# A two-block transformer and graph-attention kernel: first V spread through a mask over all partitions, four turned exponentials, identity products in TensorE's early holes, and a new order of the work

## The reference

```
cmod = silu(c) @ w_ada + b_ada            # six vectors per batch: shift, scale, gate, twice
x_mod = ln(x) * (1 + scale) + shift
k, q, v = split(x_mod @ w_qkv)
w = softmax((q / 8) k^T)                  # per batch and head, 32 x 32
x = x + gate * ((w v) @ w_proj + b_proj)
x = x + gate2 * (gelu(modulate(ln(x)) @ w_mlp1 + b_mlp1) @ w_mlp2 + b_mlp2)
```

```
self = concat(x, q_exp) @ W_self.T + b_self       # q_exp is zeroed where a row of x sums to 0
A = adj or its transpose, columns 0 to 19; label_bias = A @ w_bias + b_bias
aff = (self Wq)(self Wk)^T / sqrt(8), masked where A.sum(-1) == 0, + label_bias
output += softmax(aff) @ kv @ Wout + bout          # for each d
result = x + relu(self + output of both directions)
```

## Time and profile before

| what | value |
|---|---|
| runs | 101.66, 102.17, 102.39 us; median 102.17 us |
| profiled run | 101.14 us, span 99.3 us |
| PE busy | 83.0 us (84%) |
| PEld busy | 57.8 us (58%) |
| DVE busy | 76.3 us (77%) |
| ACT busy | 65.9 us (66%) |
| POOL busy | 65.5 us (66%) |
| DMA | 5.04 MB, nearly all of it in the first 17 us, and the stores at the end |

### The profile page before, as it was taken

How to read it: one execution, slowest core, us unless ns; L and a number is a source line. 1 busy time by engine, 2 the same in 40 slices (tenths; PEclk the granted TensorE clock), 3 DMA queues, 4 the chain that set the end, 5 groups by cost and what they waited for, 6 DMA issues and landing times.

```text
span 99.3 us, 4622 instructions
## 1 busy us (share of the span) xinstructions
PE 83.0 (84%) x1894; PEld 57.8 (58%) x1894; DVE 76.3 (77%) x209; ACT 65.9 (66%) x130; POOL 65.5 (66%) x118
## 2 busy tenths in 40 slices
PE   3996898448887598997989999998999999978730
PEld 3985675244455256863755666656665857856520
DVE  1698598629999999998467994775279786999990
ACT  1928679995872717672662788899953299997520
POOL 6758799995008970999946867990201999966700
PEclk9999589999999999999999999999999999999998
DMA  2947992000000000000000000000000000000033
GB/s 48 297 145 304 436 400 81 0 3 10 3 7 0 7 0 0 7 0 0 7 0 0 0 7 0 7 0 7 0 7 3 7 0 7 10 0 7 7 106 106
DMA packets 2532, 5.04 MB, mean 51 GB/s; under 512 B 336, under 2 KB 1872, under 8 KB 2256
## 3 DMA queue, kind: packets, MB, share of 16 engines
q1 hardware_dynamic: 2080, 4.23, 11.8%
q10 hardware_dynamic: 432, 0.52, 1.5%
HBM read 4.23 MB, written 0.52 MB: 48 GB/s over the span
## 4 chain that ended last, share of the span: by engine, by line
PE 31%; DVE 25%; ACT 15%; POOL 12%; issue 12%; ACTq 2%; DVEq 0%; POOLq 0%
DVE rden_T L964 5%; PE ps_p L613 5%; PE ps_p L679 5%; POOL Vz L477 4%; PE ps_s L667 4%; ACT Vz L778 3%; PE ps_p L701 3%; PE ps_p L552 2%; PE ps_p L590 2%; DVE E L953 2%; DVE neg_max L942 2%; POOL rstd L455 2%; ACT Kb L726 2%; ACT hidden L731 2%; DVE tok L981 2%
## 5 line engine op out<-in xcount | busy, mean ns | idle before, releaser
L784 ACT ACTIVATE PT<-ps_p 128x512 f32<-128x512 f32 x24 | 14.1, 595 | 9.5 <-PE ps_p L679 7.6
L778 ACT ACTIVATE Vz<-V_turned 20x384 f32<-20x384 f32 (+4 forms) x40 | 18.0, 455 | 1.7 <-DVE V_turned L862 0.9
L520 POOL TENSOR_TENSOR E<-E,neg_max 128x320 f32<-128x320 f32 x16 | 11.6, 730 | 11.3 <-DVE neg_max L937 10.4
L679 PE MATMUL ps_p<-ident,E 128*128 128x128 f32 x96 | 15.0, 281 | 1.9 <-DVE tok L971 0.8
L679 PEld LDWEIGHTS ps_p<-ident,E 128*128 128x128 f32 x96 | 10.4, 141 | 5.2 <-issue 4.4
L528 POOL TENSOR_SCALAR Kb<-k_raw,cols,head_mask 128x240 f32<-128x240 f32 (+1 forms) x24 | 12.1, 517 | 0.5 <-ACT k_raw L744 0.5
L731 ACT ACTIVATE hidden<-ps_p,cols 128x384 f32<-128x384 f32 (+1 forms) x12 | 6.3, 543 | 5.9 <-PE ps_p L608 5.8
L448 POOL TENSOR_SCALAR var_eps<-meanvar 128x2 f32<-128x2 f32 (+2 forms) x7 | 1.4, 194 | 13.0 <-DVE meanvar L801 12.7
L929 DVE TENSOR_TENSOR E<-ps_s,bias_dir 128x320 f32<-128x320 f32 x16 | 7.7, 484 | 2.4 <-PE ps_s L667 2.3
L608 PE MATMUL ps_p<-xm,w_rest_sb 128*128 128x384 f32 (+1 forms) x24 | 8.6, 467 | 0.5 <-DVE yT L976 0.5
L964 DVE RECIPROCAL rden_T<-ps_p 128x128 f32<-128x128 f32 x8 | 7.4, 941 | 1.9 <-PE ps_p L696 1.9
(11 more groups left out here) (98 smaller groups left out, 190.7 us busy)
## 6 DMA issues: line engine op xcount, KB each, us to landing
tok<-in_adj SPq DMA_DIRECT2D x1, 1408.0 KB, 5.7
w_rest_sb<-in_w_rest SPq DMA_DIRECT2D x1, 1088.0 KB, 7.9
xT<-in_xT SPq DMA_DIRECT2D x1, 512.0 KB, 8.7
x_tok<-in_x_tok ACTq DMA_DIRECT2D x1, 320.0 KB, 4.1
w_ada_sb<-in_w_ada SPq DMA_DIRECT2D x1, 256.0 KB, 4.3
out<-x_tok SPq DMA_DIRECT2D x1, 256.0 KB, 2.4
w_qkv_sb<-in_w_qkv SPq DMA_DIRECT2D x1, 192.0 KB, 3.7
out<-x_tok SPq DMA_DIRECT2D x1, 192.0 KB, 2.1
```

Of the source, the lines that this page charges most:

```text
L520: pool.tensor_tensor(e, e, neg_max[:, i % 3, :].unsqueeze(2).broadcast_to([P, H, M]), ALU.add)\
L679: ins = pe.transpose(ps[:, j * P:(j + 1) * P], E[:, i % 3, j * HI:(j + 1) * HI, :], ident[:, :])
L778: act.activation(Vz[rows, g0 * UB:g1 * UB, d, :, q * C:(q + 1) * C], V_turned[layer + d][rows, g0 * UB:g1 * UB, :, :], ACT.Copy).then_inc( ...
L784: act.activation(PT[:, i % 2, :, :], psum_of(("turn", i))[:, :].rearrange("p (j t) -> p j t", t=P), ACT.Exp)\
```

## The change

Five things are changed together.

1. The spread of V in layer 0 writes all 128 partitions: ACT copies `V_turned` with the per-partition scale `quad_mask[:, q]`, which is one on the partitions of quarter q and zero on the others. So the two fills of `Vz` for d = 0 (one on ACT, one on POOL) are gone, and the spread waits for the mask instead of for the filled `Vz`. Layer 1 writes as before. (A path that does this spread on POOL is added too, but `POOL_SPREADS` is empty.)
2. `PT` has four buffers instead of two (`PT_RING`), so `exp` of unit i waits for `values` of unit i-4.
3. `fill` entries name the entry that comes next on PE; they wait for its bank and write identity products there. There are now seven products in five entries: three before (xnT, 0), one each before (cmod, 1), (xnT, 1), (xnT, 2) and (k, 2). Before there were two in one entry.
4. `biases` moves to the head of ACT's sequence; both fills of d = 1 leave their place between label steps 10 and 11: the first goes to POOL's start, behind the fill of `E1`'s padding, the second behind label step 0.
5. `ORDER` and `BANKS` are new as a whole. Unit 7's `turn`, `exp` and `values` and with them (proj, 2) come after the second piece's (mlp1); (x2tok, 0) and (x2tok, 1) move behind `scores` 23, with `relu` 1, `relu` 3 and `ysum` 3.

```diff
+PT_RING = 4
...
-    ("zero", ("values", 0, 0)), ("masks", 0), ("stats", (0, 0)), ("zero", ("values", 0, 1)), ("silu", 0),
-    ("dense", ("cmod", 0)), ("rstd", (0, 0)), ("apply", 0), ("stats", (0, 1)), ("take", (("cmod", 0), 0)),
-    ("rstd", (0, 1)), ("apply", 1), ("zero", ("ones", 0)), ("dense", ("xnT", 0)), ("take", (("xnT", 0), 0)),
...
+    ("zero", ("pad",)), ("masks", 0), ("zero", ("values", 1, 0)), ("stats", (0, 0)), ("silu", 0), ("stats", (0, 1)),
+    ("dense", ("cmod", 0)), ("biases", 0), ("rstd", (0, 0)), ("rstd", (0, 1)), ("apply", 0),
+    ("fill", (3, "dense", ("xnT", 0))), ("dense", ("xnT", 0)), ("apply", 1), ("take", (("cmod", 0), 0)),
+    ("stats", (0, 2)), ("fill", (1, "dense", ("cmod", 1))), ("dense", ("cmod", 1)), ("take", (("xnT", 0), 0)),
...
+    ("sub", 1), ("dense", ("v", 3)), ("scores", 2), ("take", (("v", 2), 0)), ("spread", (0, 0, 0, 1)),
+    ("spread", (0, 1, 0, 3)), ("exp", 0), ("spread", (0, 0, 0, 3)), ("take", (("k", 2), 2)), ("take", (("v", 3), 0)),
+    ("max", 2), ("turn", 1), ("sub", 2), ("label", 0), ("zero", ("ones", 0)), ("take", (("k", 2), 3)),
+    ("spread", (0, 0, 0, 0)), ("take", (("k", 2), 0)), ("dense", "qz"), ("values", 0), ("recip", 0), ("mult", 0),
+    ("zero", ("values", 1, 1)), ("label", 1), ("label", 2), ("exp", 1), ("values", 1), ("scores", 3),
...
+    ("take", (("mlp1", 1, 2), 0)), ("sub", 7), ("dense", ("k1", 0, 0)), ("take", (("k1", 0, 0), 0)),
+    ("dense", ("mlp1", 1, 1)), ("dense", ("v1", 0, 0)), ("take", (("v1", 0, 0), 0)), ("take", (("mlp1", 1, 1), 0)),
+    ("keys", (0, 0)), ("edges", 0), ("turn", 7), ("dense", ("q1", 0, 0)), ("spread", (1, 0, 0, 2)), ("exp", 7),
+    ("take", (("q1", 0, 0), 0)), ("dense", ("mlp2", 1)), ("dense", ("k1", 0, 1)), ("dense", ("v1", 0, 1)),
+    ("values", 7), ("scores", 8), ("take", (("mlp2", 1), 0)), ("take", (("mlp2", 1), 1)), ("dense", ("rowsum", 1)),
+    ("take", (("k1", 0, 1), 0)), ("recip", 7), ("mult", 7), ("selfb", 0), ("badd", 8), ("max", 8),
+    ("dense", ("proj", 2)), ("take", (("rowsum", 1), 0)), ("dense", ("self", 1)), ("dense", ("q1", 0, 1)),
...
-ACT_ZEROS = [("values", 0, 0)]
+POOL_SPREADS = []
+
+ACT_ZEROS = []
...
-        PT = sb("PT", [P, 2, HJ, P])
+        PT = sb("PT", [P, PT_RING, HJ, P])
...
-            def keep_up(count):
+            def keep_up(count, ps):
...
-                    pe.matmul(ps_s[:, 0, 0:P], ident[:, :], ident[:, :], start=True, stop=True)
+                    pe.matmul(ps[:, 0:P], ident[:, :], ident[:, :], start=True, stop=True)
+
+            def fill(count, stage, i):
+                if stage == "scores":
+                    if i:
+                        pe.wait_ge(scores_read, i)
+                    keep_up(count, ps_s[:, 0, :])
+                else:
+                    name = i if stage == "dense" else (stage, i)
+                    wait_free(name)
+                    keep_up(count, psum_of(name))
...
-                    act.wait_ge(vz_ready[d], 1)
-                    rows = slice(QUAD * q, QUAD * q + (M if layer else S))
-                    act.activation(Vz[rows, g0 * UB:g1 * UB, d, :, q * C:(q + 1) * C],
-                                   V_turned[layer + d][rows, g0 * UB:g1 * UB, :, :], ACT.Copy).then_inc(v_spread, 1)
+                    place = Vz[:, g0 * UB:g1 * UB, d, :, q * C:(q + 1) * C]
+                    turned_v = V_turned[layer + d][:, g0 * UB:g1 * UB, :, :]
+                    if layer:
+                        act.wait_ge(vz_ready[d], 1)
+                        rows = slice(QUAD * q, QUAD * q + M)
+                        act.activation(place[rows], turned_v[rows], ACT.Copy).then_inc(v_spread, 1)
+                    else:
+                        act.wait_ge(masks_ready, 1)
+                        act.activation(place, turned_v, ACT.Copy, scale=quad_mask[:, q:q + 1]).then_inc(v_spread, 1)
                 elif stage == "exp":
                     act.wait_ge(turned, i + 1)
-                    if i >= 2:
-                        act.wait_ge(values_ready, i - 1)
+                    if i >= PT_RING:
+                        act.wait_ge(values_ready, i - PT_RING + 1)
```

More of the change, by code:

```diff
@@ L119 @@
-    ("turn", 3), ("max", 4), ("sub", 4), ("recip", 2), ("stats", (1, 0)), ("scores", 5), ("spread", (0, 3, 0, 2)),
-    ("exp", 3), ("max", 5), ("mult", 2), ("label", 6), ("turn", 4), ("sub", 5), ("exp", 4), ("values", 3),
-    ("values", 4), ("rstd", (1, 0)), ("take", (("x1tok", 0), 0)), ("turn", 5), ("dense", ("xn2T", 0)), ("recip", 3),
-    ("recip", 4), ("label", 7), ("mult", 3), ("mult", 4), ("scores", 6), ("take", (("xn2T", 0), 0)),
-    ("dense", ("proj", 1)), ("take", (("xn2T", 0), 1)), ("dense", ("mlp1", 0, 2)), ("exp", 5), ("max", 6),
@@ L124 @@
-    ("take", (("proj", 1), 0)), ("values", 5), ("take", (("mlp1", 0, 2), 0)), ("take", (("proj", 1), 1)),
-    ("recip", 5), ("dense", ("mlp1", 0, 1)), ("dense", ("mlp1", 0, 0)), ("take", (("mlp1", 0, 0), 0)),
-    ("take", (("mlp1", 0, 1), 0)), ("mult", 5), ("dense", ("x1tok", 1)), ("sub", 6), ("stats", (1, 1)),
-    ("dense", ("mlp1", 0, 3)), ("dense", "qz"), ("label", 8), ("scores", 7), ("turn", 6), ("max", 7),
-    ("take", (("mlp1", 0, 3), 0)), ("dense", ("mlp2", 0)), ("label", 9), ("rstd", (1, 1)), ("sub", 7),
@@ L174 @@
-    ("ya", 2), ("ya", 3), ("badd", 20), ("values", 16), ("max", 20), ("recip", 16), ("mult", 16),
-    ("spread", (1, 2, 1, 1)), ("take", (("sbtok", 0), 0)), ("values", 17), ("scores", 21), ("turn", 18),
-    ("turn", 19), ("dense", ("x2tok", 1)), ("recip", 17), ("ya", 0), ("ya", 1), ("mult", 17), ("badd", 21),
-    ("scores", 22), ("ysum", 3), ("ysum", 0), ("ysum", 1), ("max", 21), ("sub", 20), ("badd", 22), ("relu", 1),
-    ("spread", (1, 2, 1, 2)), ("spread", (1, 2, 1, 0)), ("spread", (1, 2, 0, 1)), ("sub", 21),
@@ new lines @@
+    ("dense", ("k", 3)), ("recip", 1), ("mult", 1), ("dense", ("proj", 0)), ("take", (("k", 3), 3)),
+    ("take", (("k", 3), 1)), ("turn", 2), ("exp", 2), ("max", 3), ("sub", 3), ("take", (("k", 3), 2)),
+    ("take", (("k", 3), 0)), ("scores", 4), ("take", (("proj", 0), 0)), ("take", (("proj", 0), 1)),
+    ("dense", ("x1tok", 0)), ("max", 4), ("turn", 3), ("label", 3), ("stats", (1, 0)), ("label", 4),
+    ("rstd", (1, 0)), ("values", 2), ("spread", (0, 2, 0, 0)), ("spread", (0, 3, 0, 3)), ("exp", 3),
@@ new lines @@
+    ("dense", ("q", 3)), ("label", 5), ("sub", 4), ("turn", 4), ("recip", 2), ("mult", 2), ("spread", (0, 2, 0, 2)),
+    ("values", 3), ("take", (("x1tok", 0), 0)), ("dense", ("xn2T", 0)), ("take", (("q", 3), 0)), ("recip", 3),
+    ("take", (("xn2T", 0), 0)), ("exp", 4), ("values", 4), ("scores", 5), ("take", (("xn2T", 0), 1)),
+    ("dense", ("mlp1", 0, 2)), ("label", 6), ("recip", 4), ("mult", 3), ("mult", 4), ("dense", ("proj", 1)),
+    ("max", 5), ("sub", 5), ("spread", (0, 3, 0, 2)), ("take", (("mlp1", 0, 2), 0)), ("dense", ("mlp1", 0, 1)),
@@ new lines @@
+    ("dense", ("mlp1", 0, 3)), ("take", (("mlp1", 0, 3), 0)), ("take", (("proj", 1), 0)),
+    ("take", (("mlp1", 0, 1), 0)), ("scores", 6), ("take", (("proj", 1), 1)), ("dense", ("mlp1", 0, 0)),
+    ("dense", ("x1tok", 1)), ("turn", 5), ("take", (("mlp1", 0, 0), 0)), ("stats", (1, 1)), ("max", 6),
+    ("dense", ("mlp2", 0)), ("sub", 6), ("label", 7), ("rstd", (1, 1)), ("take", (("x1tok", 1), 0)), ("turn", 6),
+    ("take", (("mlp2", 0), 0)), ("scores", 7), ("take", (("mlp2", 0), 1)), ("spread", (0, 3, 0, 0)),
@@ L187 @@
+    ("exp", 23), ("values", 23), ("ya", 6), ("ya", 7), ("recip", 23), ("mult", 22), ("mult", 23), ("ysum", 6),
+    ("ysum", 7), ("dense", ("x2tok", 2)), ("take", (("x2tok", 2), 0)), ("relu", 6), ("relu", 5), ("relu", 7),
 ]
@@ L209 @@
[L209 to L213 removed]
+    ("cmod", 0): 0, ("xnT", 0): 1, ("cmod", 1): 2, ("k", 0): 3, ("xnT", 1): 0, ("v", 0): 1, ("q", 0): 2,
@@ L771, in _ @@
                     ins.then_inc(xn_act, 1)
-                elif stage == "spread":
+                elif stage == "spread" and not on_pool(i):
                     layer, c, d, q = i
```

194 lines of the change are left out of this document (97 added, 97 removed), and 10 rows, old and new, of the table BANKS.

## The result

The changed kernel took **96.07 us** (median of four runs, 95.43 to 96.36) against 101.95 us for the kernel before (101.66 to 102.39): ratio 0.9411, 95% interval 0.9349 to 0.9473. Timed again in a later job, unaltered, it stood at 0.9483 (0.942 to 0.9547), so the gain is 5.2 to 5.9 us. The forecast was 99.3 us with a range from 97.0 to 101.9: the sign was right, the size off by half.

A forecast was written before the change was run, and what follows sets the result against it. It saw a changing bound: waits in the first 22 us, then DVE, PE, ACT, PE, PE with ACT, DVE. Gains of 2.5 + 0.3 + 0.1 = 2.9 us gave 99.3 us on the median, range 97.0 to 101.9.

The forecast's parts named there:

- the price of the mask on ACT: Layer 0's spreads on ACT: the scale operand adds 0.09 us each, 0.7 us for eight, before the first values.
- The bound of the first 22 us: Up to 22 us all engines wait for each other; largest hole, PE 2.06 and DVE 1.93 us, is for late biases.
- Start: Before ACT's second apply: first rstd about 4.2 us, first modulated chunk 0.9 us later, second apply 0.9 us earlier.
- ACT to the first values: ACT from second apply to chunk 0's last spread: 9.2 us plus 0.4 of gaps, values 0 2.7 us earlier.
- the clock: PE at 10 to 13 us: fills keep the clock from 0.50, worth 0.7 us of PE, counted at nothing.
- DVE's stage: Up to the third mlp input: DVE, 98% busy, hands the lead on less 0.7 us of waits; 2.5 us left.
- Labels: POOL's label path: two fills leave it, 3.9 us less, bias_dir about 4 us earlier, no gain in itself.
- PE's stages: From 38.8 to 79.5 us: same PE entries but one exchange, only idle can change; 0.3 us gained.
- The blocked third piece: Rival, chance 0.10: values 7 and proj 2 behind mlp2 of piece 1 make piece 2's mlp2 1.9 us late: 104.1 us.
- End: Last units: moving x2tok behind scores 23 gains 0.5 us, relus and ysum 3 lose 0.4; net 0.1 gained.
- three signs of a wrong forecast: values 0 after 20 us, PE idle over 2.5 us between 37 and 77, or scores 23 to last relu growing over 1 us.
- PE has more room: Rival, chance 0.12: all PE idle from 38.8 us goes (1.4 us), the last units give 0.9 instead of 0.1: 97.1 us.

The follow-up runs named there:

- b_mask: Kernel before with layer 0's spread through the mask (128 partitions, scale operand), both d = 0 fills gone, order otherwise the same: ratio 0.9983.
- a_nofill: Changed kernel without its seven identity (fill) products, the warm-up products at the start kept: ratio 0.9498 to the kernel before.
- the two load experiments: Changed kernel with one more reciprocal on DVE before recip 2: 0.9546; with one more identity product on PE before each of scores 3, 4, 5: 0.9485.
- b_biases: Kernel before with one entry moved, biases to the head of ACT's sequence: ratio 0.9729, 2.8 us faster.
- b_zero_early: Kernel before with the two d = 1 fills of Vz moved to before label steps 0 and 1: ratio 0.9988.
- b_relu_late: Kernel before with relu 1, 0, 3, 4 and 2 moved behind mult 21, ahead of ysum 5: ratio 1.0044.

## Why the prediction was wrong, point by point

Three terms of the sum failed: the price of the mask on ACT was put at 0.7 us and cost nothing; a wait of DVE was charged to the end, which it didn't reach; and PE's waits in the last units were left out. The points in order:

**The bound of the first 22 us: right.** The hole behind `biases` was a real one. *Start:* `rstd` at 4.22 us (4.2 forecast), `apply` 0 at 5.42 (5.5). The six fill records took 0.92 us and not 1.4, so the first modulated chunk was 0.44 us late, not 0.9. ACT's second `apply` began at 8.75 (8.7).

**ACT to the first values: mis-sized by 1.0 us, and the term is the price of the mask.** I forecast 9.2 us of work and 0.4 of gaps; it was 8.56 and none. `values` 0 came 3.68 us earlier for the forecast 2.7. I had counted the instructions rightly: 27 in the old stretch and 24 in the new, with one exponential, one key take, one spread and `biases` fewer and three key takes more. The term that failed is the 0.7 us for the scale operand of eight spreads. Their records did grow: 415 ns for 307 at 128 columns, 526 for 408, 624 for 520, that is 0.10 to 0.12 us against my 0.09, with the width going from 32 partitions to 128 as well. The rule of the Trainium skill (ScalarE: Activation LUTs, What ACT_TABLE_LOAD costs) puts a per-partition pointer operand at about 93 ns; the trace is 11 to 25 ns above it. But a longer record is not a later successor. In the changed kernel a masked spread of 128 columns is followed 0.29 us after its start and one of 256 columns after 0.40 us; the unmasked ones of the kernel before were followed after 0.21 to 0.33 and 0.31 to 0.44. The same sequence with and without the mask took 7.13 and 7.30 us (b_mask). At nothing for the mask the sum gives 8.5 us of work, and 8.56 was measured.

The 0.4 us of gaps is the other part. Of the old order's 1.7 us of ACT idle 0.88 was one wait for POOL's `neg_mean`, 0.60 one for PE's products at the clock of 0.50, and the rest small stops, mostly beside unmasked spreads. None of them is in the new profiled run. I counted the clock at nothing, since "ACT sets the pace". ACT does wait for PE where the early products are slow: 1.9 us in a_nofill, 1.77 us in the unaltered kernel's second profiled run. So the clock should have stood in the sum as a risk. How much of it the identity products take away is not shown.

**DVE's stage: this step failed.** I took 0.7 us off the lead ("2.5 us left") for waits around `rstd` (1, 1). The wait for `rstd` did not come: the take of x1tok 1 (35.70) follows `sub` 6 without a stop. Another one of the size came just ahead, at `stats` (1, 1), for PE's transposes:

```profile
33.32 0.69 DVE L838 BATCH_NORM_STATS2 stats<-ps_p 128x6 f32<-128x128 f32 x3 [0.87 <-PE ps_p L584]
...
35.70 0.87 DVE L846 SCALAR_TENSOR_TENSOR xn_tok<-ps_p,meanvar,rstd 128x128 f32<-128x128 f32 x3
```

From its first reciprocal to mlp2 of piece 0 DVE idled 1.21 us for 0.43 before, so it did lose about what I took off. (Over the whole stage the two look alike, 1.19 and 1.24 us, only because 0.76 of the old one is the end of the wait for `biases`.) What was wrong is that this loss reaches the end. DVE waited there for PE, and PE was busy without a stop from 30.15 to 35.45 us; over the stage PE idled 0.55 us less than before. That DVE paces the rest of the stage fits the two load experiments. From 2.7 to 2.5 was forecast, from 3.58 to 4.13 of PE's idle it went: 0.75 us of the miss. The other fault is of method: I carried DVE's lead from stage to stage and subtracted frictions, when PE's idle time (12.44 us in all before) was the account from which every gain had to be paid. Nor is much of a start's lead lost behind: from `values` 0 to the last relu's end the kernel before takes 75.6 us, b_biases 76.1, the changed kernel 73.7 and a_nofill 73.5, whether `values` 0 stands at 21.11, 18.86, 17.43 or 19.1.

**Labels: right.** `bias_dir` is done at 43.69 us (44 forecast). That it is no gain in itself, b_zero_early shows.

**PE's stages: right.** 0.20 us for the forecast 0.3. The blocked third piece did not happen: proj 2 is taken at 51.23 us (52.6 forecast) and mlp2 of piece 2 starts 13.85 us later, at 65.08, where I gave 14.6 and the slower rival needed 17.2 or more. The table load before `exp` 7 took the 1.28 us that I counted, and the exponential starts 0.01 us behind it (45.84).

**End: mis-sized, and the largest part of the miss.** 1.24 us of idle went where I had 0.1. The 0.4 us that I charged for the relus rested on a DVE-bound last stage, against which b_relu_late speaks. The time from `scores` 23 to the last relu even grew, from 7.64 to 7.91 us; but most of PE's waits in the last two stages of my table went. First the kernel before (74.65 to 94.9 us), then the changed one (70.9 to 89.1):

```profile
PE ps_p L679 <- DVE tok L971: 0.8, 2, 0.4
PE ps_p L701 <- ACT PT L784: 0.4, 1, 0.4
PE ps_p L679 <- POOL E L520: 0.4, 1, 0.4
PE ps_s L667 <- DVE E L929: 0.2, 1, 0.2
```

```profile
PE ps_p L736 <- ACT PT L824: 0.6, 1, 0.6
```

So `turn` and `scores` no longer wait for DVE and POOL. My sum looked at what moved work costs and left these waits out. What took them away I can't name from a single move: x2tok late costs 0.8 us in the old order. It belongs to the order of the last units as a whole, and that stays open.

**The sum.** Idle removed against forecast: 3.58 for 2.7, 0.55 for -0.2, 0.20 for 0.3, 1.24 for 0.1. That is 5.57 for 2.9. Of the 2.7 us missing, 0.9 lie before `values` 0, 0.75 in DVE's stage and 1.1 at the end. None of the three signs of a wrong forecast showed: `values` 0 stands at 17.43, PE idled 0.95 us from 37 to 77, and the tail grew by 0.27 us; they guarded only against a smaller gain. The rival "PE has more room" had the right sign but only 2.2 us more than my forecast, and I gave it 0.12.

## What to carry to other kernels

Before predicting a reordering, add up the idle time of the engine that is fullest over the whole span, cut at events and not at fixed times; a lead won ahead of stages in which some engine always works was passed on here unless a wait of that engine took it. Look first for the one entry whose result was ready long ago and which only stands late in its queue: here it was a third to half of the gain for one moved line. Price a change of an instruction by the time to the start of the next one in its queue, and not by its own record. And a busy share near one does not make an engine the bound: take work off it, and see whether the end moves.
